# Decay rows of two scans: a matmul broadcast into PSUM, and a DMA broadcast from a DRAM scratch

## What is computed

```python
cumh = cum.transpose(0, 2, 1)                 # cumulated log decay of each head
diff = jnp.where(mask, cumh[:, :, :, None] - cumh[:, :, None, :], -jnp.inf)
CB = jnp.einsum('blhn,bmhn->bhlm', C_c, B_c)
M = CB * jnp.exp(diff)                        # layer a; then M @ val
St = bt[:, :, None, None] * St + kt[..., None] * vt[:, :, None, :]   # layer b, step by step
ot = jnp.einsum('bhk,bhkv->bhv', qt, St) * gt[..., None]
```

## Time and profile before

| | |
|---|---|
| three runs | 1539.17, 1539.22, 1539.44 us (median 1539.22) |
| span of the profiled execution | 1537.1 us, 25437 instructions |
| TensorE busy | 1469.1 us (96%), 8712 matmuls |
| VectorE, ScalarE, GpSimd busy | 948.1 (62%), 837.7 (54%), 813.6 us (53%) |
| DMA | 22190 packets, 56.95 MB, mean 37 GB/s |
[...]

### The profile page before, as it was taken

One profiled execution on the slowest core, in us unless ns is written; L12 is line 12 of the kernel. 1 busy time (PEld: TensorE's weight loads), 2 busy tenths in 40 slices (PEclk: granted clock), 3 DMA queues, 4 the chain that ended last, 5 costly groups with the idle time before them and its releaser, 6 DMA issues. The chain is left out here.

```text
span 1537.1 us, 25437 instructions
## 1 busy us (share of the span) xinstructions
PE 1469.1 (96%) x8712; PEld 1275.4 (83%) x8712; DVE 948.1 (62%) x1751; ACT 837.7 (54%) x1543; POOL 813.6 (53%) x685
## 2 busy tenths in 40 slices
PE   7599999999998999999879999999999989999998
PEld 5389899898995778888679999999999986778886
DVE  5876766767665533343786767776767665434344
ACT  4265555555554433333567777777777754433332
POOL 4644444444442455555357666766666633455553
PEclk9799999999998999999999999999999989999999
DMA  2001000000001111111211111111111001111111
GB/s 98 0 22 26 21 20 24 27 24 21 22 1 38 42 42 51 46 46 31 76 35 43 48 48 34 41 48 48 34 41 48 14 1 48 42 52 41 51 43 46
DMA packets 22190, 56.95 MB, mean 37 GB/s; under 512 B 2688, under 2 KB 3584, under 8 KB 21888
## 3 DMA queue, kind: packets, MB, share of 16 engines
q1 hardware_dynamic: 22144, 56.35, 11.9%
HBM read 55.29 MB, written 1.05 MB: 37 GB/s over the span
## 5 line engine op out<-in xcount | busy, mean ns | idle before, releaser
L391 POOL TENSOR_TENSOR ms_a_lo<-m_a,ms_a_hi 128x384 fp32r<-128x384 f32 x128 | 130.5, 1020 | 218.6 <-ACT ms_a_hi L387 218.6
L1085 DVE TENSOR_TENSOR f_h<-f_sc,ps 128x512 f32<-128x512 f32 x112 | 76.3, 681 | 185.5 <-POOL f_sc L1017 185.5
L242 PE MATMUL ps<-xn_hi,fgu_hi 128*128 128x512 f32 x448 | 179.6, 401 | 5.0 <-DVE f_h L1085 5.0
L243 PE MATMUL ps<-xn_lo,fgu_hi 128*128 128x512 f32 x448 | 178.7, 399 | 0.0
L244 PE MATMUL ps<-xn_hi,fgu_lo 128*128 128x512 f32 x448 | 178.6, 399 | 0.0
L1087 DVE TENSOR_TENSOR fh_lo<-f_h,fh_hi 128x512 fp32r<-128x512 f32 x112 | 108.2, 966 | 98.9 <-ACT fh_hi L387 98.9
L966 ACT ACTIVATE f_s<-ps 128x512 f32<-128x512 f32 x112 | 66.9, 599 | 163.3 <-PE ps L244 163.1
L1017 POOL TENSOR_TENSOR f_sc<-f_s,coef_r 128x512 f32<-128x512 f32 x88 | 113.3, 1288 | 66.7 <-ACT f_s L966 66.7
L387 ACT CAST fh_hi<-f_h 128x512 fp32r<-128x512 f32 x112 | 69.1, 617 | 124.7 <-DVE f_h L1085 124.5
L242 PE MATMUL ps<-xn_hi,aw_hi 128*128 128x512 f32 x256 | 108.5, 424 | 18.2 <-DVE bmat_lo L715 18.2
L391 POOL TENSOR_TENSOR fd_lo<-fw_raw,fd_hi 128x256 fp32r<-128x256 f32 x56 | 51.5, 919 | 125.6 <-ACT fd_hi L387 125.6
(11 more groups left out here) (290 smaller groups left out, 5049.3 us busy)
## 6 DMA issues: line engine op xcount, KB each, us to landing
fw_raw<-ffn_w SPq DMA_DIRECT2D x56, 384.0 KB, 3.1
wconv_raw<-b_conv SPq DMA_DIRECT2D x16, 513.0 KB, 3.5
aw_raw<-a_heads SPq DMA_DIRECT2D x32, 256.0 KB, 2.6
wvo_raw<-b_vo SPq DMA_DIRECT2D x16, 512.0 KB, 3.4
wqk_raw<-b_qk SPq DMA_DIRECT2D x16, 256.0 KB, 2.6
x<-xT SPq DMA_DIRECT2D x2, 512.0 KB, 5.7
a_vg_raw<-a_vg SPq DMA_DIRECT2D x1, 1024.0 KB, 8.7
out<-x SPq DMA_DIRECT2D x1, 1024.0 KB, 3.9
```

Of the source, the lines that this page charges most:

```text
L242: nc.tensor.matmul(o, w[0], v[0], start=first, stop=False, skip_group_check=True)
L243: nc.tensor.matmul(o, w[0], v[1], start=False, stop=False, skip_group_check=True)
L391: return nc.gpsimd.tensor_tensor(dst[1], src, f32(dst[0]), ALU.subtract).then_inc(sem(done_sem), 1)
L1085: nc.vector.tensor_tensor(f_h[:, c], f_sc[:, c], ps[:, 2 + c, :], ALU.mult).then_inc(sem("f_h"), 1)
```

## The change

`split_pieces`, `pieces_a`, `pieces_b`, the 0/1 rows and the second half of `bounds` go. SP stores the cumulated decays in a DRAM scratch of 128x256 float32 once and, for each head and each pair of sequences, loads the two rows on all 128 partitions (256 KB, one DMA; `rows_of`). Exponents read the row from SBUF and the causal bound from 128 unused PSUM columns; they cover the two diagonal blocks alone, 128 columns each. ScalarE makes the third block from the row itself with ncum as its bias, and the exp of the other two. The decay matmuls (L466, L1235) go. In the layer-b loop the wait on `fold_split` ahead of the scores of sequence 1 goes as well.

```diff
-N_CONST = 3 * P + 32
+N_CONST = 2 * P
+        causal_ps = ps[:, 2, TRI:CHUNK]
+        a_rows_d = nc.dram_tensor("a_rows_d", (P, SEQ), F32, kind="Internal").ap()
+        b_rows_d = nc.dram_tensor("b_rows_d", (P, SEQ), F32, kind="Internal").ap()
-        pieces_a = sb(ma2, "pieces_a", [P, BATCH, TRI], BF16)
+        rows_a = sb(ma2, "rows_a", [P, CHUNKS, 2, SEQ])
...
-            pe.wait_ge(sem("a_pieces"), PIECES)
-            pe.wait_ge(sem("a_ncum"), 1)
...
-            d, s = ps[:, 2 + u % 2, :], ps[:, 4 + u % 2, :]
-            lhs = rows_b[:, bass.ds(g * A_GROUP + j, 1)].broadcast_to([P, P])
-            nc.tensor.matmul(d[:, 0:TRI], lhs, pieces_a[:, b, :], start=True, stop=True, skip_group_check=True).then_inc(sem("a_d_done"), 1)
+            s = ps[:, 4 + u % 2, :]
...
-                nc.scalar.activation(e_a[:, u % 2], e_a[:, u % 2], ACT.Exp).then_inc(sem("a_e_done"), 1)
+                decays_act(e_a[:, u % 2], rows_a[:, b // 2, b % 2, :], ncum_a, b, h).then_inc(sem("a_e_done"), 1)
...
-            dve.wait_ge(sem("a_cum"), 1)
-            step(nc.vector.tensor_copy(dec_z[:], dec_e[:]))
-            split_pieces(dve, step, pieces_a, dec_z[:], dec_p, "a_pieces")
             a_conv_dve(dve, step, 2)
...
             dve.wait_ge(sem("a_val"), A_TILES)
+            dve.wait_ge(sem("a_pro_read"), len(A_PRODUCTS))
+            nc.vector.tensor_copy(causal_ps, causal).then_inc(sem("a_causal"), 1)
+            dve.wait_ge(sem("a_causal"), 1)
...
+        def rows_of(rows_d, h, c):
+            return rows_d.rearrange("(b h) l -> h b l", b=BATCH)[bass.ds(h, 1), 2 * c:2 * c + 2, :].broadcast_to([P, 2, SEQ])
...
-            nc.vector.scalar_tensor_tensor(first_m(e), first_m(d), ncum[:, 2 * b, bass.ds(h, 1)], bounds, ALU.add, ALU.min)
-            return nc.vector.scalar_tensor_tensor(e[:, P:2 * P], d[:, P:2 * P], ncum[:, 2 * b + 1, bass.ds(h, 1)],
-                                                  bounds[:, 0], ALU.add, ALU.min)
+        def exponents_dve(e, row, ncum, b, h):
+            for d in range(2):
+                ins = nc.vector.scalar_tensor_tensor(e[:, d * P:(d + 1) * P], row[:, d * P:(d + 1) * P], ncum[:, 2 * b + d, bass.ds(h, 1)],
+                                                     causal_ps, ALU.add, ALU.min)
+            return ins
+        def decays_act(e, row, ncum, b, h):
+            nc.scalar.activation(e[:, 2 * P:TRI], row[:, P:SEQ], ACT.Exp, bias=ncum[:, 2 * b, bass.ds(h, 1)])
+            return nc.scalar.activation(e[:, 0:2 * P], e[:, 0:2 * P], ACT.Exp)
...
-                dve.wait_ge(sem("a_d_done"), UNITS * g + u + 1)
+                dve.wait_ge(sem(f"a_rows_loaded{b // 2}"), 16 * A_GROUP * g + 16 * j + 16)
                 dve.wait_ge(sem("a_ncum"), 1)
+                if u >= 2:
+                    dve.wait_ge(sem("a_m_done"), UNITS * g + u - 1)
...
+            sp.wait_ge(sem("a_cum"), 1)
+            sp.dma_start(a_rows_d, dec_e[:]).then_inc(sem("a_rows_stored"), 16)
+            sp.wait_ge(sem("a_rows_stored"), 16)
+            for c in range(CHUNKS):
+                sp.dma_start(rows_a[:, c], rows_of(a_rows_d, 0, c)).then_inc(sem(f"a_rows_loaded{c}"), 16)
             with sp.Fori(0, A_TILES - 1) as g:
...
+                for c in range(CHUNKS):
+                    if not (last and j == A_GROUP - 1):
+                        sp.wait_ge(sem("a_e_done"), UNITS * g + j * BATCH + 2 * c + 2)
+                        sp.dma_start(rows_a[:, c], rows_of(a_rows_d, g * A_GROUP + j + 1, c)).then_inc(sem(f"a_rows_loaded{c}"), 16)
...
-                pe.wait_ge(sem("b_pieces"), PIECES)
-            if b == 1 and not last:
-                pe.wait_ge(sem("fold_split"), h + 2)
-            nc.tensor.matmul(d[:, 0:TRI], lhs, pieces_b[:, b, :], start=True, stop=True, skip_group_check=True).then_inc(sem("b_d_done"), 1)
...
-            split_pieces(dve, step, pieces_b, bg_z[:, 1], bg_p, "b_pieces", [0, 1])
             b_make_dve(dve, 0, 0, ["conv1"])
-            split_pieces(dve, step, pieces_b, bg_z[:, 1], bg_p, "b_pieces", [2])
...
+        def b_rows_sp(sp, h):
+            for c in range(CHUNKS):
+                sp.wait_ge(sem("b_e_done"), BATCH * h + 2 * c + 2)
+                sp.dma_start(rows_b[:, c], rows_of(b_rows_d, h + 1, c)).then_inc(sem(f"b_rows_loaded{c}"), 16)
```

More of the change, by code:

```diff
@@ L91, in build_layer @@
         ident = const[:, 0:P]
-        bounds = const[:, P:3 * P].rearrange("p (d l) -> p d l", d=2)
-        rows_b = sb(ctx, "rows_b", [P, 32], BF16)
+        causal = const[:, P:2 * P]
         mean_w = sb(ctx, "mean_w", [P, P])
@@ L195, in build_layer @@
         wconv = pair(mb, "wconv0", [P, 2, B_TAPS, P]), wconv1
-        pieces_b = sb(mb, "pieces_b", [P, BATCH, TRI], BF16)
+        rows_b = sb(mb, "rows_b", [P, CHUNKS, 2, SEQ])
         ncum_b = sb(mb, "ncum_b", [P, BLOCKS, 32])
@@ L652, in a_early_dve @@
             nc.vector.memset(yT[:, CHUNK:], 1.0).then_inc(sem("y_gated"), 2)
-            nc.vector.memset(pieces_a[:], 0.0).then_inc(sem("a_early"), 1)
             nc.vector.memset(neg_a[:], 0.0).then_inc(sem("y_read"), 2)
-            dve.wait_ge(sem("a_early"), 2)
+            dve.wait_ge(sem("a_early"), 1)
         def a_conv_dve(dve, step, t):
@@ L743, in a_group_dve @@
                 j, b = u // BATCH, u % BATCH
-                dve.wait_ge(sem("a_d_done"), UNITS * g + u + 1)
+                dve.wait_ge(sem(f"a_rows_loaded{b // 2}"), 16 * A_GROUP * g + 16 * j + 16)
                 dve.wait_ge(sem("a_ncum"), 1)
-                exponents_dve(e_a[:, u % 2], ps[:, 2 + u % 2, :], ncum_a, b, g * A_GROUP + j).then_inc(sem("a_bounded"), 1)
+                if u >= 2:
+                    dve.wait_ge(sem("a_m_done"), UNITS * g + u - 1)
+                exponents_dve(e_a[:, u % 2], rows_a[:, b // 2, b % 2, :], ncum_a, b, g * A_GROUP + j).then_inc(sem("a_bounded"), 1)
                 if u > 0 and not (last and u > UNITS - BATCH):
@@ L1227, in b_score_pe @@
                 pe.wait_ge(sem("b_conv_y"), 4 * h + 4)
-                pe.wait_ge(sem("b_pieces"), PIECES)
-            if b == 1 and not last:
-                pe.wait_ge(sem("fold_split"), h + 2)
-            d, s = ps[:, 2 + u, :], ps[:, 4 + u, :]
+            s = ps[:, 4 + u, :]
             if b % 2 == 0:
                 pe.wait_ge(sem("qk_split"), 4 * h + 3 + b // 2)
-            lhs = rows_b[:, bass.ds(h, 1)].broadcast_to([P, P])
-            nc.tensor.matmul(d[:, 0:TRI], lhs, pieces_b[:, b, :], start=True, stop=True, skip_group_check=True).then_inc(sem("b_d_done"), 1)
             mm3(first_m(s), at(qk[p], slice(None), 1, slice(l0, l0 + P)), halves(at(qk[p], slice(None), 0, slice(l0, l0 + SEQ))), True, False)
@@ L1377, in b_score_act @@
             act.wait_ge(sem("b_bounded"), BATCH * h + b + 1)
-            nc.scalar.activation(e_b[:, b % 2], e_b[:, b % 2], ACT.Exp).then_inc(sem("b_e_done"), 1)
+            decays_act(e_b[:, b % 2], rows_b[:, b // 2, b % 2, :], ncum_b, b, h).then_inc(sem("b_e_done"), 1)
         def b_head_act(act, h, p, last, weights):
@@ L1417, in b_dve @@
             step(nc.vector.memset(bg_ones[:], 1.0))
-            step(nc.vector.memset(pieces_b[:], 0.0))
+            step(nc.vector.tensor_copy(causal_ps, causal))
             dve.wait_ge(sem("b_params"), 16)
@@ L1438, in b_dve @@
             dve.wait_ge(sem("b_cum"), 1)
-            step(nc.vector.tensor_tensor(bg_z[:, 1], bg_z[:, 1], bg_cum[:], ALU.add))
+            nc.vector.tensor_tensor(bg_z[:, 1], bg_z[:, 1], bg_cum[:], ALU.add).then_inc(sem("b_row"), 1)
             b_make_dve(dve, 0, 0, ["conv0"])
@@ L1495, in b_exponents_dve @@
         def b_exponents_dve(dve, h, b):
-            dve.wait_ge(sem("b_d_done"), BATCH * h + b + 1)
+            dve.wait_ge(sem(f"b_rows_loaded{b // 2}"), 16 * h + 16)
             dve.wait_ge(sem("b_ncum"), 1)
-            exponents_dve(e_b[:, b % 2], ps[:, 2 + b % 2, :], ncum_b, b, h).then_inc(sem("b_bounded"), 1)
+            if b >= 2:
+                dve.wait_ge(sem("b_m_done"), BATCH * h + b - 1)
+            exponents_dve(e_b[:, b % 2], rows_b[:, b // 2, b % 2, :], ncum_b, b, h).then_inc(sem("b_bounded"), 1)
         def b_score_dve(dve, h, b):
@@ L1615, in b_sp @@
                 sp.dma_start(raw[:], src[P:2 * P, :]).then_inc(sem(f"{name}_loaded"), 16)
+            sp.wait_ge(sem("b_row"), 1)
+            sp.dma_start(b_rows_d, bg_z[:, 1]).then_inc(sem("b_rows_stored"), 16)
+            sp.wait_ge(sem("b_rows_stored"), 16)
+            for c in range(CHUNKS):
+                sp.dma_start(rows_b[:, c], rows_of(b_rows_d, 0, c)).then_inc(sem(f"b_rows_loaded{c}"), 16)
             with sp.Fori(0, B_HEADS - 2) as h:
@@ L1619, in b_sp @@
                     sp.dma_start(raw[:], src[bass.ds(h * P + 2 * P, P), :]).then_inc(sem(f"{name}_loaded"), 16)
+                b_rows_sp(sp, h)
+            b_rows_sp(sp, B_HEADS - 2)
+        def b_rows_sp(sp, h):
+            for c in range(CHUNKS):
+                sp.wait_ge(sem("b_e_done"), BATCH * h + 2 * c + 2)
```

(1 more changed line is left out.)

6 lines of the change are left out of this document (removed).

## The result

The changed kernel takes **1513.2 us** (median of 4 runs, 1511.5 to 1513.8) where the kernel before takes 1539.2 on the same chip: ratio 0.983, 95% interval 0.982 to 0.984. The profiled run took 1511.5 us for a span of 1509.7, so 27.4 us of span went; the granted clock of TensorE is 0.988 in the mean over it, 0.982 in the kernel before. The forecast was 38.7 and 1500.5 us. The stages tell where the 11 us of difference are. Each row is the distance of two starts of TensorE in the two time lines: the first value product of a loop, and the first matmul of a norm (`ps<-x,mean_w`).

The account below looks back on a forecast made before the run. TensorE's instruction stream was taken to bound both loops, VectorE's `split_pieces` to delay the prologues. Gains 10.4 + 8.5 + 14.3 + 5.5 = 38.7 us; 1537.1 - 38.7 + 2.1 = 1500.5 us, range 1490 to 1513.

Parts of the forecast that it names:

- Part 1: First prologue: without `split_pieces` the last convolution ends at 60.6 instead of 71.18 us; net 10.4 us, bounds 6 and 14.
- what is late next: First prologue, after the convolution: TensorE restarts on its low clock, nothing won; bound and stage copies cost 0.0 to 0.4 us.
- Part 2: Second prologue: without `split_pieces` TensorE's 7.20 us wait at the fold vanishes; 8.5 us, bounds 6.6 and 9.
- Part 3, loop 1: First loop: 128 fewer decay matmuls, 124 units counted at 0.13 us, less 1.8 at group starts; 14.3 us gained.
- loss of 0.46 per group: Loop 1's group starts: two decay matmuls' gain lost (0.26 us) and ScalarE's longer exp (0.2), four times: -1.8 us.
- Part 3, loop 2: Second loop: 64 fewer decay matmuls; batches 2 and 3 gain 3.9 us over 15 heads, last head 1.6; sum 5.5.
- Part 4: Replacement work in the loops: VectorE 0.14 us less per unit, off the path; ScalarE's two exps 0.2 us more.
- costs only at the chain places: Both loops: ScalarE's extra 0.2 us per unit is covered by its idle time, except at the chain places.
- DMA: 96 new 256 KB row loads, taken as 3 us each; they and the weight load behind them are covered.
- rival (c): Row loads become the bound: from 7.3 us load time each of 32 heads grows; 1587 us at 10; chance 0.05.
- (a): Rival forecasting 1489 us, below which the range's low end was set; chance 0.08.
- (b): Rival: ScalarE's 0.2 us is paid in most units, loops give nothing, only prologues count; 1520 us, chance 0.10.

Follow-up runs that it names:

- e10: Changed kernel plus e5 and e4, loop 1's 128-column exponential ahead of its wait and the causal bound copied before `stage`: 1498.7 us.
- e7: Kernel before without cutting the decay rows into pieces in both prologues (decays left out of the result), 17 empty instructions keeping the loop's place: 1518.5 us.
- e5: Changed kernel with 19 empty VectorE instructions ahead of its first loop, putting it where the kernel before has it: 1504.8 us.
- e6: e5 with a 384-column decay product put back per unit of loop 1 as idle work: 1516.8 us.
- e1: Changed kernel with the head of VectorE's first loop placed at slot 0 of an instruction block: 1503.6 us.
- e4: Changed kernel with loop 2's 128-column exponentials on ScalarE taken out of the pair and made early: 1510.2 us.
- e8: e5 with the first loop's rows loaded once and used by all heads (their own decays left out): 1503.3 us.
- e2: Changed kernel with the head of VectorE's first loop placed at slot 64 of an instruction block: 1511.6 us.
- e3: Kernel before with only the head of VectorE's first loop placed at slot 64: 1544.5 us against 1538.6.
- e9: Changed kernel with a jump hint on VectorE's first loop (`hint_back_edge`), one instruction more, loop's place kept: 1504.3 us.

## Why the prediction was right in direction and 12.7 us off

The time fell as forecast, but by 27.4 of 38.7 us of span. That the median lies at the edge of the range is luck: its upper end was made of the prologues' bounds and 5 us for the loops in general, and the largest loss, 8.4 us in loop 1, comes from a mechanism that the prediction doesn't have.

**Part 1 (10.4 forecast, 9.3 measured).** The contention argument held to 0.2 us: the three L659 take 9.42 us beside GpSimd, 9.12 were taken, and L698 starts at 60.40. The missing microsecond is at the end. Bound copy, stage copy, ScalarE's SiLUs and its table load (1.28 us) stood in the sum with 0.0 to 0.4. In the trace they end in a wait of TensorE of 1.44 us for the first masked block: VectorE copies the bound at 68.81, waits 0.87 us for that copy and has the exponents only at 70.58. With the bound copied early (e10) that wait is 0.59, and ScalarE then starts its exponential at 70.20, straight behind its table load: what is late next is ScalarE. The step "what is late next" stopped at TensorE's clock. e7 puts the price of the pieces at 9.7 with the copy ahead of them left in.

**Part 2 (8.5 forecast, 8.1 measured; 8.4 in e7).** Right, with its reason: the wait at the fold is gone, the one for ScalarE's q grew from 0.99 to 1.86, where 1.7 was worked out.

```profile
770.12 0.50 PE L243 MATMUL ps<-xn_hi,wqk_hi 128*128 128x512 f32 x1 [1.86 <-ACT q L1321]
```

**Part 3, loop 1 (14.3 forecast, 6.0 measured).** The term itself was right: with the stalls away (e5) it is 14.3, e6 puts 13.9 back, and TensorE waits 0.69 us for `valz_lo` at a group's start instead of 0.24, as the forecast's loss of 0.46 per group said. What failed is a step that isn't in the sum at all. It treated the change as work on the engines' paths; the change also moves and lengthens code, and that cost 8.4 us by e5, of which the forecast has nothing, not even in a rival. The wait and the clock that follows are 4.9 us at the first jump and 5.1 at the second (periods 98.9 and 99.1 against 94.0), 10.0 together; the changed kernel gets 1.6 of them back in its last group. What the runs show of it is the packets at 164.6, 167.0 and 169.7 us beside a stall of 4.67 us, and both gone from another place (e1, e5). How many instructions a block holds, or how many of a loop's 348 or 356 stay with the engine, no run shows, and the kernel before, without a gap at its jumps, gave no hint that the loop's place could cost anything.

**Part 3, loop 2 (3.6 forecast for 14 heads, 1.3 measured).** The step that failed is the one that charged ScalarE's pair of exponentials in loop 1 only. The decay products of batches 2 and 3 do count, and the 0.26 us that they free ahead of the wait for `ms_b_lo` was to lengthen it from 0.20 to near 0.5. It is 0.63, because the chain that ends there contains the pair: from the start of the exponents to the value product 3.73 us before (831.88 to 835.61) and 3.85 after (838.39 to 842.24). VectorE's exponents at the start of that chain, in the kernel before and in the changed one:

```profile
831.88 0.47 DVE L726 SCALAR_TENSOR_TENSOR e_b<-ps,ncum_b,const 128x256 f32<-128x256 f32 x1
...
838.39 1.11 DVE L709 SCALAR_TENSOR_TENSOR e_b<-rows_b,ncum_b,ps 128x128 f32<-128x128 f32 x4
```

With the second exponential out of the chain (e4) a head takes 30.37 us, 0.34 less than before instead of 0.10. So what Part 4 said "costs only at the chain places" belonged into loop 2 as well, once per head: 14 x 0.12 = 1.7 us by the chain's length, which leaves 1.9 of the 3.6; the other 0.6 us isn't settled. In the last head the first value product came 3.49 us behind the end of TensorE's wait for `qk_lo` (1227.29 to 1230.78) instead of 4.66 before (1252.74 to 1257.40): 1.17, where 1.1 was worked out. The rest of its 1.7 us isn't settled; e7 shows that the clock alone moves this stage by 1.8.

**Part 4.** Exponents 339 ns against 342; the pair 0.40 each and 0.71 from start to end (e.g. 1212.64 to 1213.35), inside 0.65 to 0.75. The 128-column one, with its per-partition bias, costs the 0.30 + 0.1 that the prediction allowed, the 256-column one the 0.41, and they overlap by 0.1 as assumed. The price was right; only the places where it is paid were missed.

**DMA.** 4.8 us to land instead of the 3 taken, and the weights behind them 5.1, as worked out. Both hidden (e8): rival (c) needed 7.3.

**Rivals.** (a), whose 1489 us set the range's low end, charged a decay product 0.16 us, a price that no run shows; e6 shows 0.12 and refutes it. (b), the chains as the bound, was right in the second loop in part and wrong in the first. (c) is refuted by e8. The 8.4 us of loop 1 came from none of them.

## What to carry to other kernels

An edit to a loop also moves the code of every engine that it touches: where a loop has a few hundred instructions on an engine (348 and 356 here), look for idle time named "issue" at its top and for instruction packets on the DMA queues there, before and after, and keep range for it (here 5.9 to 8.4 us for two jumps). A price per instruction taken from start distances (0.13 us) held in the runs (0.12), and the longer record (0.34) or the column count (0.17, an estimate) did not. An instruction that gets longer "off the path" still has to be looked for in every chain in which a wait ends, also when the loop as a whole is bound elsewhere; and one that needs less than its partner can stand ahead of the wait (3 us here).

## What the runs showed of the hardware that was not expected

- The same loop of 348 or 356 VectorE instructions runs without a gap or with a stall of 2.5 to 4.9 us at each jump back, by its place alone (e1, e2, e3, e5). With the stall, 9 or 10 packets of 8 KB pass on the instruction queue in two iterations; without it, none.
- The stall's length is 4.67 and 4.93 us in the changed kernel and 2.46 to 2.68 in e2 and e3. It goes with the packets: after a jump they pass 2.4 to 2.8 us apart, and two of them fall within the stall of the changed kernel, one within those of e2 and e3. Why one more is needed there is open.
- A hint on the jump removes it at both jumps (e9), at the cost of one instruction and of 1.12 us of "issue" at the loop's entry.
- Entering a placed loop cost 3.24 us of VectorE in e1 and 3.22 in e2, but nothing in e3; 19 empty instructions cost nothing that can be measured (e5).
- Row loads in pieces of 1 KB raise the landing time of the loads in the same queue from 2.6 to 5.1 us (4.9 in e5), though the group periods stay the same to 0.1 us without them (e8).
